# A four-layer graph network on one core: where the edge attributes are summed

## What is computed

```python
# layer 0: messages, summed by destination
messages = relu(concat([x[row], x[col]]) @ W_msg + b_msg)
aggregated = segment_sum(messages, col)
h = relu(concat([x, aggregated]) @ W_upd + b_upd)      # then a layernorm
# layer 1: edge attributes (53125 x 96), reduced by destination
out1 = segment_sum(edge_attr, col)
cnt  = segment_sum(ones, col)
out2 = where(cnt > 0, segment_max(edge_attr, col), 0)
out3 = out1 / maximum(cnt, 1)
h = relu(concat([x, out1, out2, out3, u[batch]]) @ W1 + b1) @ W2 + b2
```

## Time and profile before

| | |
|---|---|
| runs (3) | median 2780.43 us, 2780.08 to 2782.35 |
| the profiled execution | 2774.67 us, its span 2772.6 us |
| message pass, first gather to last accumulation | 132.9 to 670.3 us |
| attributes' pass, first scan to last store | 769.9 to 1090.4 us |
| busy over the span | PE 49%, PEld 39%, DVE 57%, ACT 24%, POOL 52% |

### The profile page before, as it was taken

How to read it: one execution, slowest core, us unless ns; L and a number is a source line. 1 busy time by engine, 2 the same in 40 slices (tenths; PEclk the granted TensorE clock), 3 DMA queues, 4 the chain that set the end, 5 groups by cost and what they waited for, 6 DMA issues and landing times. The chain is left out here.

```text
span 2772.6 us, 26946 instructions
## 1 busy us (share of the span) xinstructions
PE 1354.4 (49%) x7570; PEld 1068.0 (39%) x7570; DVE 1589.9 (57%) x3262; ACT 674.0 (24%) x1528; POOL 1436.7 (52%) x1444
## 2 busy tenths in 40 slices
PE   3677787888589999979990000000001411111104
PEld 2466676777389997545660000000000300000003
DVE  2467777776689998532224666666665344443342
ACT  1112222212457775111120000000002233333331
POOL 2177777776300000301016777777754377777774
PEclk9789999999789999989995555555555655555557
DMA  2487777773166663010004566666651466666664
GB/s 80 129 242 230 234 238 235 234 236 102 47 164 155 153 156 92 26 10 14 9 16 122 190 190 197 191 196 194 194 181 53 132 208 209 211 211 211 211 210 135
DMA packets 272030, 433.06 MB, mean 156 GB/s; under 512 B 108749, under 2 KB 181031, under 8 KB 271883
## 3 DMA queue, kind: packets, MB, share of 16 engines
q1 hardware_dynamic: 202635, 247.61, 27.1%
q0 software_dynamic: 66784, 183.09, 24.5%
q10 hardware_dynamic: 2464, 0.64, 0.1%
HBM read 302.15 MB, written 128.80 MB: 155 GB/s over the span
## 5 line engine op out<-in xcount | busy, mean ns | idle before, releaser
L1753 POOL DMA_INDIRECT att_rows<-att_table,lane_source x416 | 463.2, 1113 | 126.7 <-issue 126.7
L2079 POOL DMA_INDIRECT best_rows<-message_source_table,lane_source x416 | 393.5, 946 | 167.2 <-issue 126.4
L735 POOL DMA_INDIRECT msg_rows<-message_source_table,msg_index x416 | 399.6, 961 | 146.4 <-issue 126.5
L2190 DVE SCALAR_TENSOR_TENSOR best_state<-best_state,lane_line,best_ps_rows 128x256 f32<-128x256 f32 x416 | 199.8, 480 | 316.3 <-ACT best_ps_rows L2104 298.0
L1785 PE MATMUL att_ps_upto<-ident,att_largest 128*4 128x128 f32 x1 | 0.4, 375 | 608.0 <-DVE att_largest L1850 608.0
L863 PE MATMUL msg_ps_sum<-msg_by_edge,msg_rows 128*128 128x128 f32 x1664 | 229.9, 296 | 110.2 <-DVE aggT L795 108.5
L863 PEld LDWEIGHTS msg_ps_sum<-msg_by_edge,msg_rows 128*128 128x128 f32 x1664 | 215.2, 208 | 142.2 <-issue 141.1
L2104 ACT ACTIVATE best_ps_rows<-best_rows,lane_weight 128x256 f32<-128x256 f32 x416 | 173.5, 462 | 359.4 <-DMA best_rows<-message_source_table,lane_source 359.4
L2138 PE MATMUL best_ps_self<-w_selfT,hT 128*125 128x256 f32 x100 | 51.7, 671 | 398.7 <-DVE x L2196 387.4
L1785 PEld LDWEIGHTS att_ps_upto<-ident,att_largest 128*4 128x4 f32 x1 | 0.1, 82 | 608.8 <-DVE att_largest L1850 608.8
L847 PE MATMUL msg_ps_window<-msg_window,msg_by_node 128*128 128x256 f32 x832 | 211.0, 400 | 22.7 <-DMA msg_window<-message_window_table 20.0
(11 more groups left out here) (290 smaller groups left out, 2713.8 us busy)
## 6 DMA issues: line engine op xcount, KB each, us to landing
att_states<-aggT SPq DMA_DIRECT2D x104, 528.0 KB
msg_window<-message_window_table SPq DMA_DIRECT2D x416, 128.0 KB
best_states<-best_state SPq DMA_DIRECT2D x104, 512.0 KB
attr_rows<-in_edge_attr SPq DMA_DIRECT2D x103, 192.0 KB, 3.3
msg_line<-place_line SPq DMA_DIRECT2D x52, 256.0 KB, 4.8
attr_line<-mask_line SPq DMA_DIRECT2D x52, 256.0 KB, 4.0
attr_carry<-carry_line SPq DMA_DIRECT2D x52, 256.0 KB
msg_rows<-message_source_table,msg_index POOLq DMA_INDIRECT x416
```

The source lines that it names most:

```text
L735: nc.gpsimd.indirect_dma_start(rows[:, s, t, :], None, table, bass.IndirectOffsetOnAxis(ap=index[:, s, t:t + 1], axis=0)).then_inc(self.ro ...
L1753: nc.gpsimd.indirect_dma_start(rows[:, t % ring, :], None, self.attention_table, bass.IndirectOffsetOnAxis(ap=self.lane_source[:, t:t + 1] ...
L2079: nc.gpsimd.indirect_dma_start(rows[:, g % SLOTS, t, :], None, table, bass.IndirectOffsetOnAxis(ap=self.lane_source[:, g * TG + t:g * TG + ...
L2190: nc.vector.scalar_tensor_tensor(out=state[:, g % STATE_BUFS, t, :], in0=before, scalar=self.lane_line[:, n:n + 1], in1=weighed_row(n), op ...
```

## The change

The sums of the attributes and the edge counts move from the attributes' pass into the message pass. There SP also fetches the group's attributes into a new tile of 128 x 128 per edge tile, whose column 96 holds ones; PE makes a third product per tile; an accumulation covers three blocks of aggT in place of two. PE signals each tile's sums singly, and each tile has one PSUM bank, so that a tile's products wait for the accumulation of the same tile of the group before. In DVE's turn the fourth accumulation comes in front of add, and the second half of by_edges between the third and fourth. The attributes' pass loses the carry line (in `opening` too, with one step of DVE and one store), the second scan, and half of the transposes back, of the products and of the columns that ACT copies; ACT's two halves become one copy, and the PSUM tile between them gets a second buffer. `mlp` reads the sums from block 2 and has its scratch in block 1. The branches for an attention and a gathered maximum, which no call used, are dropped.

```diff
-    def sum_pass(self, name, table, width, window_table, window_width, attention, ahead=None):
+    def message_pass(self, ahead):
...
+            edges = self.sb("msg_edges", [P, BUFS, TG, P], ctx=ctx)
-            ps_sum = [self.ps(f"{name}_ps_sum{b}", [P, TG, blocks, P], ctx) for b in range(2)]
+            ps_sum = [self.ps(f"msg_ps_sum{t}", [P, 3, P], ctx) for t in range(TG)]
+            def tiles_upto(g, t=TG - 1):
+                return g * TG + t + 1
...
+                    def fetch_edges(i, s):
+                        g = i * SLOTS + s
+                        if g >= BUFS:
+                            sp.wait_ge(summed, tiles_upto(g - BUFS))
+                        self.fetch_attributes(sp, edges[:, s % BUFS, :, :], attributes_in[s % BUFS], g)
-                    pipelined(sp, [(fetch_index, 3), (fetch_window, 0)])
+                    pipelined(sp, [(fetch_index, 3), (fetch_window, 0), (fetch_edges, 0)])
...
+                    nc.gpsimd.memset(edges[:, :, :, AF:AF + 1], 1.0).then_inc(ones_made, 1)
+                    nc.gpsimd.memset(edges[:, :, :, AF + 1:P], 0.0).then_inc(ones_made, 1)
...
                     def by_edges(i, s, half):
+                        if half == 1 and i * SLOTS + s >= BUFS:
+                            dve.wait_ge(summed, tiles_upto(i * SLOTS + s - BUFS))
...
                     def accumulate(i, s, t):
-                            dve.wait_ge(ev["summed"], self.ready(i, s))
-                        self.after_tile_before(dve, tile_added, i, s, t)
-                        at = self.aggT[:, 0:blocks, bass.ds(bases[t], P)]
+                        n = tiles_upto(i * SLOTS + s, t)
+                        dve.wait_ge(summed, n)
+                        if n > 1:
+                            dve.wait_ge(tile_added, n - 1)
+                        at = self.aggT[:, :, bass.ds(bases[t], P)]
...
-                        pipelined(dve, [(acc[0], 0), (by_nodes, 5), (acc[1], 0), (hot[0], 4), (hot[1], 4), (acc[2], 0),
-                                        (add, 3), (acc[3], 0)])
+                    pipelined(dve, [(acc[0], 0), (by_nodes, 5), (acc[1], 0), (hot[0], 4), (acc[2], 0), (hot[1], 4),
+                                    (acc[3], 0), (add, 3)])
...
                     def gather_sums(i, s):
+                        pe.wait_ge(*self.attributes_landed(attributes_in[s % BUFS], g))
                         pe.wait_ge(ev["weighed"], self.ready(i, s))
-                        pe.wait_ge(tile_added[TG - 1], self.freed(i, s, 2))
                         for t in range(TG):
+                            if g > 0:
+                                pe.wait_ge(tile_added, tiles_upto(g - 1, t))
...
+                            nc.tensor.matmul(ps_sum[t][:, 2, :], edges[:, s % BUFS, t, :], by_edge[:, s % BUFS, t, :],
+                                             start=True, stop=True).then_inc(summed, 1)
...
-    def max_pass(self, name, outT, table=None, ahead=None, first=None):
+    def attribute_max_pass(self, outT, ahead):
...
-                        for k in range(nk):
-                            sums = attributes and k == 1
-                            last = nc.vector.tensor_tensor_scan(
-                                scan[:, s % 2, k, :], (carry if sums else line)[0:bw, s % BUFS, :],
+                        dve.wait_ge(ev["back"], self.freed(i, s, 2))
+                        nc.vector.tensor_tensor_scan(scan[:, s % 2, :], line[0:AF, s % BUFS, :], ps_turned[s % 2][:],
...
-                        stages.insert(1, (keep(act, nc.scalar.copy, 0, HALF), 2))
-                        stages.insert(3, (keep(act, nc.scalar.copy, HALF, HALF), 2))
+                    stages = [(of_tile(store, t), 0) for t in range(TG)]
+                    stages.insert(2, (keep, 2))
```

More of the change, by code:

```diff
@@ L57 @@
 HID = 1024
-SPLIT = 3
 H_BITS = 2
@@ L689, in sum_pass @@
         with ExitStack() as ctx:
[L690 to L702, removed]
-            ps_sum = [self.ps(f"{name}_ps_sum{b}", [P, TG, blocks, P], ctx) for b in range(2)]
+            index = self.sb("msg_index", [P, SLOTS, TG], I32, ctx)
+            rows = self.sb("msg_rows", [P, SLOTS, TG, D], ctx=ctx)
@@ new lines, in attribute_max_pass @@
+            rows = self.sb("attr_rows", [P, SLOTS, TG, AF], ctx=ctx)
+            line = self.sb("attr_line", [P, BUFS, GE], BF16, ctx)
+            scan = self.sb("attr_scan", [AF, 2, GE], ctx=ctx)
+            by_edge = self.sb("attr_by_edge", [P, BUFS, TG, AF], ctx=ctx)
+            ends = self.sb("attr_ends", [P, BUFS, TG, P], ctx=ctx)
+            ps_turned = [self.ps(f"attr_ps_turned{b}", [AF, GE], ctx) for b in range(2)]
+            ps_back = [self.ps(f"attr_ps_back{b}", [P, TG, AF], ctx) for b in range(2)]
@@ L937, in _ @@
-                    pipelined(sp, [(fetch_attributes if attributes else fetch_index, 3), (mask, 0)])
-                if attributes:
-                    @block.gpsimd
-                    def _(pool):
-                        nc.gpsimd.memset(rows[:, :, :, AF:AF + 1], 1.0).then_inc(ones_made, 1)
-                        if ahead:
-                            self.load(pool, *ahead)
-                if not attributes:
-                    @block.gpsimd
-                    def _(pool):
-                        def gather(i, s):
-                            hold(pool, *self.landed(self.index_in, i, s, groups=PAIR), least=16)
-                            hold(pool, ev["turned"], self.freed(i, s, SLOTS))
-                            for t in range(TG):
-                                nc.gpsimd.indirect_dma_start(
-                                    rows[:, s, t, :], None, table,
-                                    bass.IndirectOffsetOnAxis(ap=index[:, s, t:t + 1], axis=0)
-                                ).then_inc(self.rows_in[s], 16)
-                        pipelined(pool, [(gather, 0)])
@@ L978, in _, with keep @@
+                    pipelined(sp, [(fetch_edges, 3), (mask, 0)])
+                @block.gpsimd
+                def _(pool):
+                    self.load(pool, *ahead)
                 @block.scalar
                 def _(act):
-                    self.start_events(act, [ev["kept"] if attributes else ev["weighed"]] + stored)
-                    def weigh(i, s, t):
-                        if t == 0:
-                            rows_landed(act, i, s)
-                        w = self.weight[:, bass.ds(i * (SLOTS * TG) + (s * TG + t), 1)]
-                        last = nc.scalar.activation(rows[:, s, t, :], rows[:, s, t, :], ACT.Copy, scale=w)
-                        if t == TG - 1:
-                            last.then_inc(ev["weighed"], 1)
+                    self.start_events(act, [ev["kept"]] + stored)
+                    def keep(i, s):
+                        act.wait_ge(ev["back"], self.ready(i, s))
+                        act.wait_ge(ev["placed"], self.freed(i, s, BUFS))
+                        nc.scalar.copy(by_edge[:, s % BUFS, :, :], ps_back[s % 2][:]).then_inc(ev["kept"], 1)
@@ L1239, in mlp_weights, with mlp @@
         return (w1, w2, b1, b2, u0, parts), (transfers, self.sem("mlp_loads"))
-    def mlp(self, edgesT, weights, transfers, loads):
+    def mlp(self, maxT, sums, weights, transfers, loads):
         w1, w2, b1, b2, u0, parts = weights
```

263 lines of the change are left out of this document (70 added, 193 removed).

## The result

| | before | after |
|---|---|---|
| median of 4 runs, us | 2780.26 (2778.51 to 2782.35) | 2873.11 (2869.84 to 2876.32) |
| ratio, 95% interval | | 1.0334 (1.0316 to 1.0352) |
| the profiled execution, span | 2774.67, 2772.6 | 2876.32, 2874.5 |
| opening, to the first gather | 132.9 | 130.8 |
| message pass, first gather to end of last accumulation | 537.4 | 754.3 |

The rows of the table add up to the difference of the spans: -2.1 + 216.9 - 3.9 - 111.6 + 2.7 = 102.0 us. The attributes' pass won what it was expected to win, and the message pass lost twice as much.

The account below looks back on a forecast made before the run. POOL's gathers bound the message pass, DVE and PE the attributes' pass. +215 us for the late line and -111 us for the attributes' pass with its start make +104, so 2884 us; way 2 gives 2845 to 2913, all cases 2795 to 2945.

Parts of the forecast that it names:

- The bound before: Message pass of the kernel before: POOL's gathers set the pace, 1.265 us each, 5.06 us a group.
- The line is late by the order of SP's program: Message pass: the line, behind fetch_edges' wait for sums in SP's program, is late for 49 even groups, 6 to 102.
- The loop of 14.5 us: Message pass, two groups from by_nodes to by_nodes: 14.5 us against 10.12, 49 times, +215 us.
- The landing: Message pass: the line of places takes 4.4 us from issue to landing, with 3.6 and 5.6 as ends.
- Half clock after the stall: Message pass: PE runs partly at 1.2 GHz after 3.4 us idle; each stall costs about 1.6 us more.
- way 2: Message pass, PE at half clock after its stall: loop of 14.5 us, +215 us; chance 0.54.
- way 1: Message pass, PE at full clock: loop of 13.1 us, +146 us, 2815 us in total; chance 0.24.
- The work itself: Message pass, work a group: DVE about 4.1 us, PE 4.68, an accumulation 0.54; both engines fit under 5.06.
- The transfers: Message pass: attributes add 0.8 to 1.5 us a group to 4.0; under 0.8 of the engines at the slower pace, no cost.
- The attributes' pass: Attributes' pass: a turn falls from 3.01 to 1.97 us, ACT tightest at 1.95; 108 us less over 104 turns.
- The term of 3 us for a shorter start: Start of the attributes' pass: without the carry line the scans wait less, 3 us gained, between 0 and 8.
- The faster rival: Message pass: the line isn't late and POOL keeps the pace; only the attributes' gain is seen, 2669 us; chance 0.08.

Follow-up runs that it names:

- both leads: Kernel after with index lead 5 and windows and lines lead 2, in place of 3 and 0: 0.9591 of the kernel before, 2661.63 us; 0.9663 on a slow chip.
- first eight runs: Eight edits of the kernel after, four on each of two chips; measured ratios to the kernel before from 0.9598 to 1.0505.

## Why the prediction was right

It gave +104 us and 2884; measured were +102 us between the profiled executions and 2873 as the median. The last 5.8 us that it added for the median over the profiled execution of before did not carry over: the profiled execution of after is the longest of its four.

- **The bound before** (POOL's pace) was right: with the line in time, that pace comes back.
- **The line is late by the order of SP's program.** Right in place and in number: 49 even groups were named, 51 waits were measured, two of them at the start of the pass and 49 from 158.84 us on. They are longer than the 4 to 5 us each that were named as a sign: 5.1 to 7.8 for most, 6.0 on average. Issued earlier, the line is waited for less, issued later, more.
- **The loop of 14.5 us** measured 14.6. Its terms: by_nodes to the end of the sums 9.3 forecast, 9.0 measured (497.44 to 506.46); wake-up and attribute transfer 0.48 and part of the 0.3, measured 0.31 + 0.49; landing, seen from by_nodes, 4.4 and the rest of the 0.3, measured 4.86. So an expansion was 0.27 us too dear (1.62 in place of 1.89) and the last terms 0.48 too cheap in all (0.31 + 0.49 + 4.86 for 0.48 + 4.4 + 0.3). The sum was better than its parts.
- **The landing** of the line was 3.6 / 4.2 / 5.8 us (least, median, most), against 4.4 taken. The estimate of 2.6 us from the Trainium skill, "DMA: Bandwidth & Descriptors", section "Anatomy of one DMA", is below the least again.
- **Half clock after the stall.** Right, and the one term that a run has measured by itself: 69 us, and way 2 less way 1 was 215 - 146 = 69 in the prediction. In the loop shown, tiles two to four take 3.62 us behind the stall (498.44 to 502.06) and three tiles take 2.01 at full clock (504.45 to 506.46): 1.6 us, the term. The stall is 4.17 us where 3.4 were worked out. The Trainium skill's "TensorE: Matmul & The Clock Gate", section "What's actually happening", has the penalty of the ramp below 1% of a typical kernel's span. Here slow work behind stalls costs 69 of 2873 us, 2.4%, as it comes back 49 times and stands in the ring that sets the pace. The sentence speaks of a typical kernel and not of stalls that come back, so the prediction took it too widely when it had it speak against the term.
- **The work itself**: accumulation 0.54 forecast, 0.545 measured (L758); a DVE turn with no wait 505.24 - 501.04 = 4.2 for 4.1; a group on PE at full clock 4.4 (502.06 to 506.46) for 4.68.
- **The transfers** were oversized for the fast pace. Share times pace is 0.91 x 4 x 1.281 = 4.66 us a group with both leads, against 4.8 to 5.5: there the attributes add 0.66 us to the 4.0 of before and not 0.8 to 1.5. In the kernel after it is 0.67 x 7.3 = 4.89, at the lower end of the forecast. It cost nothing, as the slow pace left room, and even at the old pace the engines are not full.
- **The attributes' pass**: a turn of 1.97 forecast and 1.961 measured; a store 0.27 for 0.265 (L879), the joint copy 0.49 for 0.478 (L869). But the turn came out right partly by luck. The prediction named ACT the tightest, at 1.95 us (its terms add up to 1.92), and PE well below. In the trace no scan waits for ACT, which is busy for 104 of 150 us, while DVE is busy for 142 and PE for 143. DVE's own 1.84 us is the bound, and what comes on top is waits for mask lines, 9.3 us in 16 of them behind the first, with little else. The chain of ACT was mis-sized in its waits for the copy before: three of 0.13 us a turn forecast, 22.5 us in all measured, 0.2 a turn. The term of 3 us for a shorter start measured 3.9 (99.6 less 95.7), of which the first scan's wait for its line gives 2, from 21.3 to 19.3 us. From the last accumulation to the last store the pass won 115.5 us (3.9 + 111.6), and 111 were forecast.
- **The faster rival** was the kernel that the change might have been: 2669 us with only the attributes' gain. The two leads give 2662.

## What to carry to other kernels

Before a transfer that waits is put into an engine's program, write down what stands behind it: a wait on a queue's engine holds up every later issue, whatever buffers these have. When such a transfer reuses a buffer that is freed late, give the stages that others depend on a longer lead; one line of the stage list was worth 7.3% here. Read an experiment that moves a load of transfers by each wait and not by their sum: a wait that comes back elsewhere looks like no effect. And price a stall of TensorE with the slow loads behind it where the stall comes back in the loop that sets the pace.

## What was not expected of the hardware

On the two chips of the first eight runs the kernel before took 2982 and 2990 us, 7.4 to 7.7% more than the 2775 to 2780 of the others, with the same program. The traces of the edited kernels show where to look. SP's register move ahead of a window's issue (least/median/most ns, first and last start) in the kernel with both leads, on such a chip:

```profile
L696 SPq MOVE msg_window<-message_window_table x416: 2/29/1396, 125.7 to 775.8; - x139
```

and in the same kernel on a chip of the common speed:

```profile
L696 SPq MOVE msg_window<-message_window_table x416: 29/29/42, 122.9 to 641.9; - x139
```

A move that never takes more than 42 ns takes up to 1396 there. Waits also end there at an event for which the profile names no instruction; in the same kernel, from 200 to 750 us:

```profile
DVE aggT L758 <- remote: 87.0, 47, 3.9
```

The same kernel starts its last accumulation at 800.8 us there and at 672.0 here. What takes the time, whether something shares the core's paths or its instruction supply, stays open: it was not tried, and no run of the kernel before on such a chip has a trace. What the ratios say is less hurt by it than the times: both leads give 0.9663 there and 0.9591 here.
